# A graph network on one core: split-precision attention scores, a full-precision second weight layer on row halves, softmax numbers stored in rows of 512, and an earlier scatter of the carries

## What is computed

```python
wk = mlp2(edge_features, k_w1, k_b1, k_w2, k_b2)     # relu(x @ w1 + b1) @ w2 + b2
wv = mlp2(edge_features, v_w1, v_b1, v_w2, v_b2)
k = tensor_product(x_dst, edge_sh, wk, Cqk)          # sum_s sh[e,s] * (x_e @ C[:,s,:]) * w
v = tensor_product(x_dst, edge_sh, wv, Cv)
attn = einsum('ehd,ehd->eh', q[edge_src], k)         # 8 heads of 16
ex = exp(attn - segment_max(attn)[edge_src])
alpha = ex / (segment_sum(ex)[edge_src] + 1e-16)
upd = segment_sum(v * alpha) @ W_out
out = batchnorm(x @ W_self + upd)                    # then a residual and a layer norm
```

## Time and profile before

| | before |
|---|---|
| median of 3 runs | 2948.41 us (2947.21 to 2949.53) |
| profiled execution: time, span | 2947.53 us, 2945.7 us |
| mean granted TensorE clock over the span | 0.899 |
| busy in the span: PE, DVE, ACT, POOL | 2469.1, 2612.7, 1514.6, 1731.3 us |

### The profile page before, as it was taken

One profiled execution on the slowest core, in us unless ns is written; L12 is line 12 of the kernel. 1 busy time (PEld: TensorE's weight loads), 2 busy tenths in 40 slices (PEclk: granted clock), 3 DMA queues, 4 the chain that ended last, 5 costly groups with the idle time before them and its releaser, 6 DMA issues.

```text
span 2945.7 us, 48186 instructions
## 1 busy us (share of the span) xinstructions
PE 2469.1 (84%) x12310; PEld 1787.3 (61%) x12505; DVE 2612.7 (89%) x3389; ACT 1514.6 (51%) x2914; POOL 1731.3 (59%) x1719
## 2 busy tenths in 40 slices
PE   2233347999999999999999999999999999999714
PEld 1233315677777776777677776777677777777511
DVE  6688835899999999999999999999999999999737
ACT  1321224566666655666566665666566566666310
POOL 1800037777777766667676666666666677665030
PEclk7555557999999999999999999999999999999855
DMA  6787714245555544444444444444445544544340
GB/s 187 202 222 187 210 25 111 76 131 149 148 149 145 148 147 139 141 142 148 139 144 142 146 147 140 140 144 147 142 141 147 148 141 142 148 144 132 121 124 11
DMA packets 282407, 415.35 MB, mean 141 GB/s; under 512 B 64463, under 2 KB 191875, under 8 KB 278470
## 3 DMA queue, kind: packets, MB, share of 16 engines
q1 hardware_dynamic: 222278, 296.67, 32.4%
q0 software_dynamic: 52704, 107.19, 15.1%
q10 hardware_dynamic: 7128, 8.13, 0.8%
HBM read 309.59 MB, written 102.20 MB: 140 GB/s over the span
## 4 chain that ended last, share of the span: by engine, by line
PE 52%; DVE 7%; issue 6%; ACT 3%; DMA 2%; POOL 2%; SPq 0%; DVEq 0%; ACTq 0%; POOLq 0%
PE bank L1118 11%; PE bank L1120 9%; PE bank L1119 9%; PE bank L1142 5%; PE bank L1163 4%; PE bank L1194 2%; PE bank L1124 2%; PE bank L1125 2%; PE bank L1095 2%; PE bank L1113 2%; DVE xa_t L1538 1%; DVE z_l L1546 1%; PE bank L1102 1%; POOL gathered L745 1%; PE bank L1101 1%
## 5 line engine op out<-in xcount | busy, mean ns | idle before, releaser
L745 POOL DMA_INDIRECT gathered<-xtab_d,src_g x784 | 780.6, 996 | 449.7 <-PE bank L1095 203.0
L745 POOL DMA_INDIRECT gathered<-qtab_d,dst_g x784 | 801.9, 1023 | 257.2 <-issue 249.0
L1118 PE MATMUL bank<-z_h,wt_h 128*128 128x512 f32 x1568 | 729.6, 465 | 27.9 <-DVE val L1578 27.9
L1538 DVE TENSOR_TENSOR xa_t<-bank,r_r 128x512 f32<-128x512 f32 x980 | 667.3, 683 | 13.5 <-PE bank L1142 10.3
L876 ACT ACTIVATE z_h<-xa_t 128x512 fp32r<-128x512 f32 x980 | 617.4, 634 | 110.1 <-DVE xa_t L1538 100.3
L1120 PE MATMUL bank<-z_h,wt_l 128*128 128x512 f32 x1568 | 620.7, 396 | 0.0
L1119 PE MATMUL bank<-z_l,wt_h 128*128 128x512 f32 x1568 | 618.8, 395 | 0.0
L1546 DVE TENSOR_TENSOR z_l<-xa_t,z_h 128x1024 fp32r<-128x1024 f32 x392 | 478.0, 1219 | 48.2 <-ACT z_h L876 44.6
L1118 PEld LDWEIGHTS bank<-z_h,wt_h 128*128 128x128 f32 x1568 | 301.1, 192 | 131.4 <-issue 92.7
L869 ACT ACTIVATE hid<-bank,b1kv 128x512 f32<-128x512 f32 x196 | 134.8, 688 | 476.4 <-PE bank L1102 462.4
L1120 PEld LDWEIGHTS bank<-z_h,wt_l 128*128 128x128 f32 x1568 | 294.9, 188 | 69.2
(11 more groups left out here) (222 smaller groups left out, 4057.9 us busy)
## 6 DMA issues: line engine op xcount, KB each, us to landing
nrow_d<-x_r SPq DMA_DIRECT2D x196, 288.0 KB
ea<-in_ea_t SPq DMA_DIRECT2D x392, 128.0 KB
exb<-exd_d SPq DMA_DIRECT2D x392, 128.0 KB
dmb<-exd_d SPq DMA_DIRECT2D x392, 128.0 KB
ea_c<-in_ea_t SPq DMA_DIRECT2D x49, 512.0 KB, 5.0
aggrow_d<-xa_t SPq DMA_DIRECT2D x49, 512.0 KB, 3.9
gathered<-xtab_d,src_g POOLq DMA_INDIRECT x784
gathered<-qtab_d,dst_g POOLq DMA_INDIRECT x784
```

Of the source, the lines that this page charges most:

```text
L745: rows_in = pool.indirect_dma_start(rows[:, c % 4, k, :], None, table, bass.IndirectOffsetOnAxis(ap=picked[:, s, at:at + 1], axis=0))
L1118: pe.matmul(ps[:, :], wt_h[rows, w, :], high, start=start, stop=False)
L1538: dve.tensor_tensor(z[:, i, :], bank[2 + (NJ * c + i) % 2][:, :], xt[:, c % 2, :], ALU.mult).then_inc(z_ok, 1)
```

## The change

1. **Second weight layer.** `weights` no longer uses rounded parts. Two plain fp32 matmuls of 256 edges for the keys and two for the values, in turn, replace the six rounded ones of 512. `hid_h` (ScalarE) and `hid_l` (VectorE) are gone, and the matmuls wait for `hid` alone.
2. **Scores.** `kq` is now split: `scores_high` (ScalarE, new) rounds it to `kq_h`, `scores_low` (VectorE, new) takes the remainder `kq_l`, and four rounded matmuls of 256 replace two plain fp32 ones. `kq` has one buffer in place of two.
3. **Softmax numbers.** The rows of the batch are ordered half first, then group, then head. `exd_d` holds rows of 512. A batch is stored by four DMAs of 56 rows (before: two of 112), and a group's `exb` and `dmb` are loaded by two DMAs with rows of 512 (before: four with rows of 256). The reset flags are loaded by two DMAs per batch (before: one).
4. **Tail.** The carries are scattered after 12 of the 25 gathers (before: 16).

```diff
@@ tiles
-        kq = in_h(P, 2 * G).rearrange("p (b g) -> p b g", b=2)
+        kq = in_h(P, G)
...
@@ load_rs
-                sp.dma_start(rs_b[:, s % 2, :], ... .to_broadcast([NPC, H, HG])).then_inc(rs_in[s % 2], 16)
+                for f in range(2):
+                    sp.dma_start(rs_b[f * BG * H:(f + 1) * BG * H, s % 2, :], flags[f].to_broadcast([BG, H, HG])
+                                 ).then_inc(rs_in[s % 2], 16)
@@ store_exponents
                 for k, tile in enumerate((b_att, b_dec)):
-                    sp.dma_start(exd_d[bass.ds(j * (UNROLL // BG) + s, 1), k].rearrange("o i f h w -> (o i f h) w"),
-                                 tile).then_inc(exd_out[s % 2], 16)
+                    for f in range(2):
+                        sp.dma_start(exd_d[bass.ds(j * (UNROLL // BG) + s, 1), k, :, :, f * HG:(f + 1) * HG]
+                                     .rearrange("o g h w -> (o g h) w"), tile[f * BG * H:(f + 1) * BG * H, :]
+                                     ).then_inc(exd_out[s % 2], 16)
@@ load_exponents
                 for k, tile in enumerate((exb, dmb)):
-                    for f in range(2):
-                        sp.dma_start(tile[:, c % 2, f * HG:(f + 1) * HG], ... .to_broadcast([H, DH, HG]))
+                    sp.dma_start(tile[:, c % 2, :], ... .to_broadcast([H, DH, G])).then_inc(exd_in[c % 2], 16)
@@ tail, GpSimd
-            gather_ends(range(0, 16))
+            gather_ends(range(0, 12))
...
-            gather_ends(range(16, NT))
+            gather_ends(range(12, NT))
@@ ScalarE
-                act.activation(hid_h[:, :], ps_hw[:, :], ACT.Relu, bias=b1kv[:, :]).then_inc(hid_ok, 1)
+            def scores_high(j, c):
+                done(act, kq_ok, j, c)
+                past(act, att_ps, j, c, 1)
+                act.activation(kq_h[:, :], kq, ACT.Copy).then_inc(kqh_ok, 1)
@@ TensorE, weights
-                done(pe, hidl_ok, j, c)
+                done(pe, hid_ok, j, c)
...
-                for ps, rows, done_ps in ((ps_xw, slice(0, D), wk_ps), (ps_hw, slice(D, P), wv_ps)):
-                    split_matmul(ps, W2KV, hid_h[rows, :], hid_l[rows, :], True, True, rows).then_inc(done_ps, 1)
+                for f in range(2):
+                    edges = slice(f * HG, (f + 1) * HG)
+                    mk = pe.matmul(ps_xw[:, edges], w2kv[0:D, :], hid[0:D, edges], start=True, stop=True)
+                    mv = pe.matmul(ps_hw[:, edges], w2kv[D:P, :], hid[D:P, edges], start=True, stop=True)
@@ TensorE, scores
-                done(pe, kq_ok, j, c)
+                done(pe, kql_ok, j, c)
...
-                    mm = pe.matmul(ps_att[0:BP, 0:HG], head_sel[:, BP - H - H * i:2 * BP - H - H * i],
-                                   kq[:, c % 2, f * HG:(f + 1) * HG], start=i == 0, stop=i == NPC - 1)
+                    for part in (kq_h, kq_l):
+                        mm = pe.matmul(ps_att[0:BP, 0:HG], head_sel[:, BP - H - H * i:2 * BP - H - H * i],
+                                       part[:, f * HG:(f + 1) * HG], ...)
@@ VectorE
-                dve.tensor_tensor(hid_l[:, :], hid[:, :], hid_h[:, :].bitcast(F32), ALU.subtract
-                                  ).then_inc(hidl_ok, 1)
-                past(dve, att_ps, j, c, 2)
-                dve.tensor_tensor(kq[:, c % 2, :], ps_k[:, :], qt[:, c % 2, :], ALU.mult).then_inc(kq_ok, 1)
+                past(dve, kql_ok, j, c, 1)
+                dve.tensor_tensor(kq, ps_k[:, :], qt[:, c % 2, :], ALU.mult).then_inc(kq_ok, 1)
+            def scores_low(j, c):
+                done(dve, kqh_ok, j, c)
+                past(dve, att_ps, j, c, 1)
+                dve.tensor_tensor(kq_l[:, :], kq, kq_h[:, :].bitcast(F32), ALU.subtract).then_inc(kql_ok, 1)
```

More of the change, by code:

```diff
@@ L27 @@
 NJ = 5
-CK, CV, W2KV, W1KV = 0, NJ, 2 * NJ, 2 * NJ + 1
-NW = 2 * NJ + 2
+CK, CV, W1KV = 0, NJ, 2 * NJ
+NW = 2 * NJ + 1
 H = 8
@@ L82, in gnn_two_layers @@
         nrow_d = dram("nrow_d", [EP, RW])
-        exd_d = dram("exd_d", [NB, 2, BG, 2, H, HG])
+        exd_d = dram("exd_d", [NB, 2, BG, H, G])
         carry_d = dram("carry_d", [NP + PIECES, RW])
@@ L102, in gnn_two_layers @@
         wt_l = sb("wt_l", [P, NW, O], F32R)
-        head_sel = sb("head_sel", [P, 2 * BP - H])
+        w2kv = sb("w2kv", [P, O])
+        head_sel = sb("head_sel", [P, 2 * BP - H], F32R)
         chain_cut = sb("chain_cut", [P, PIECES])
@@ L228, in gnn_two_layers @@
         hid = sb("hid", [P, G])
-        hid_h = sb("hid_h", [P, G], F32R)
-        hid_l = sb("hid_l", [P, G], F32R)
+        kq_h = sb("kq_h", [P, G], F32R)
+        kq_l = sb("kq_l", [P, G], F32R)
         qt = sb("qt", [P, 2, G])
@@ L398, in gnn_two_layers @@
         zl_ok = sem("zl_ok")
-        hidl_ok = sem("hidl_ok")
         wth_ok = sem("wth_ok")
@@ L403, in gnn_two_layers @@
         kq_ok = sem("kq_ok")
+        kqh_ok = sem("kqh_ok")
+        kql_ok = sem("kql_ok")
         val_ok = sem("val_ok")
@@ L603, in load_exponents @@
                 hold()
-                sp.wait_ge(exd_out[c // BG % 2], j * (UNROLL // BG // 2 * 32) + (c // BG // 2 + 1) * 32)
+                sp.wait_ge(exd_out[c // BG % 2], j * (UNROLL // BG // 2 * 64) + (c // BG // 2 + 1) * 64)
                 hold()
                 for k, tile in enumerate((exb, dmb)):
-                    for f in range(2):
-                        sp.dma_start(tile[:, c % 2, f * HG:(f + 1) * HG],
-                                     exd_d[bass.ds(j * (UNROLL // BG) + c // BG, 1), k, c % BG, f]
-                                     .rearrange("o h w -> (o h) w").rearrange("h (o w) -> h o w", o=1)
-                                     .to_broadcast([H, DH, HG])).then_inc(exd_in[c % 2], 16)
+                    sp.dma_start(tile[:, c % 2, :],
+                                 exd_d[bass.ds(j * (UNROLL // BG) + c // BG, 1), k, c % BG]
+                                 .rearrange("o h w -> (o h) w").rearrange("h (o w) -> h o w", o=1)
+                                 .to_broadcast([H, DH, G])).then_inc(exd_in[c % 2], 16)
             def store_row(j, c):
@@ L915, in rows @@
                 done_batch(act, bturn_ok, j, c // BG, 4)
-                act.activation(row[:, c % 2, :, O:RW],
-                               b_turn[:, c // BG % 2, c % BG * 2:c % BG * 2 + 2, :, :]
-                               .rearrange("p f h w -> p (f h) w"), ACT.Copy).then_inc(row_ok, 1)
+                act.activation(row[:, c % 2, :, O:RW].rearrange("p (f h) w -> p f h w", f=2),
+                               b_turn[:, c // BG % 2, bass.ds(c % BG, 2, BG), :, :], ACT.Copy).then_inc(row_ok, 1)
             def body(j, c):
@@ L938, in body @@
                     batch_turned(j, s)
+                if live(j, c - 1):
+                    scores_high(j, c - 1)
                 if live(j, c + 1):
@@ L1161, in scores @@
                 for f in range(2):
-                    i = c % BG * 2 + f
-                    mm = pe.matmul(ps_att[0:BP, 0:HG], head_sel[:, BP - H - H * i:2 * BP - H - H * i],
-                                   kq[:, c % 2, f * HG:(f + 1) * HG], start=i == 0, stop=i == NPC - 1)
+                    i = f * BG + c % BG
+                    for part in (kq_h, kq_l):
+                        mm = pe.matmul(ps_att[0:BP, 0:HG], head_sel[:, BP - H - H * i:2 * BP - H - H * i],
+                                       part[:, f * HG:(f + 1) * HG], start=c % BG == 0 and f == 0 and part is kq_h,
+                                       stop=c % BG == BG - 1 and f == 1 and part is kq_l)
                 mm.then_inc(att_ps, 1)
@@ L1555, in edge_low @@
                                   ALU.subtract).then_inc(eal_ok, 1)
-            def hidden_low(j, c):
-                done(dve, hid_ok, j, c, 2)
-                past(dve, wv_ps, j, c, 1)
-                dve.tensor_tensor(hid_l[:, :], hid[:, :], hid_h[:, :].bitcast(F32), ALU.subtract
-                                  ).then_inc(hidl_ok, 1)
             def key_query(j, c):
@@ L1607, in weigh_values @@
             def weigh_values(j, c):
-                landed(dve, exd_in, j, c, 64)
+                landed(dve, exd_in, j, c, 32)
                 done(dve, val_ok, j, c)
@@ L1642, in body @@
                     batch_sums(j, s)
+                if live(j, c - 1):
+                    scores_low(j, c - 1)
                 if live(j, c + 1):
```

19 lines of the change are left out of this document (9 added, 10 removed).

## The result

The change takes the median from 2947.9 to 2942.4 us: 5.5 us less, ratio 0.9978, 95% interval [0.9969, 0.9987]. The prediction was 38 us off, to 2910, so the direction was right and the size was seven times too big. The profiled execution of after took 2940.88 us.

What follows compares the result with a forecast made beforehand. TensorE was taken to bound most of the loop, with VectorE close behind; 28 us in the loop, 5 in the drain and 5 in the tail came off the profiled 2947.5, giving a median of 2910 us, range 2886 to 2943.

Steps and rivals of the forecast that it cites:

- Scores and weights: TensorE's body: score matmuls of 0.12 save 0.38 us, the second weight layer costs 0.16 more, 11.43 to 11.21.
- The strict order: Weight layer: matmuls start strictly in program order, five slots, +0.22 us; in a rival at 2938 us, chance 0.14.
- the lost overlap: Rival, weight layer: plain fp32 doesn't overlap on row halves, TensorE's body 12.08, 3036 us; chance 0.15.
- In the batch's third body that room is taken: ScalarE: batch evacuations fill its idle room, so the new 0.6 us rounding pushes `wv` and two `z_h` back.
- VectorE becomes the bound: Rival, loop: `key_query` wait and ScalarE's delay take the slack, bodies near 11.3, gain 11 us, 2927; chance 0.13.
- The wait at `key_query`: VectorE, ordinary bodies: a new wait of about 0.1 us for the weights, coming out of 0.31 of slack.
- nothing moves, by some other wait in the loop: Rival, loop: some other wait eats the gain, time near 2946 us; chance 0.03.
- Softmax numbers in the drain: End of loop: two loads a group instead of four make six rounds shorter, 5 us gained (1 to 8).
- The 1.0 a round: End of loop: gain taken for each of six rounds, 6 us in all, less 0.85 for two more stores.
- Tail: After the loop: four gathers go behind the scatter, which starts 5.0 us earlier; gain 5 us, or 3.
- 28 + 5 + 5: Whole kernel: 28 us from the loop (1.0 per batch), 5 from the drain, 5 from the tail; 38 in all.
- strict order or slow loads: Rival, TensorE: five weight slots or score matmuls 0.177 apart, body near 11.43, only ends gain, 2938; chance 0.14.

Runs made afterwards that it cites:

- `only_scores`: The kernel before with the split scores alone (hid_h and hid_l stay): 2996.54 us, ratio 1.0168.
- `only_weights`: The kernel before with the fp32 second weight layer alone: 2965.33 us, ratio 1.0059.
- run 1: The changed kernel with scores_high moved ahead of batch_turned on ScalarE: 2936.15 us, ratio 0.9956.
- run 3, the two moves: The changed kernel with scores_high ahead of batch_turned on ScalarE and scores_low ahead of key_query on VectorE: 2929.35 us, ratio 0.9935.
- Run 2: The changed kernel with only scores_low moved ahead of key_query on VectorE: 2951.96 us, ratio 1.0022.
- the control: The kernel before with three gathers of x rows per group in place of four (output incomplete): 2943.88 us, ratio 0.9988.
- run 7: The changed kernel with scores_high and scores_low moved earlier and three gathers of x rows per group in place of four (output incomplete): 2909.29 us, ratio 0.9870.
- run 5: The changed kernel with three gathers of x rows per group in place of four (output incomplete): 2922.31 us, ratio 0.9913.
- run 15: The changed kernel with scores_high and scores_low moved earlier and each 128x1024 z_l subtraction made as two of 128x512 side by side: 2906.85 us, ratio 0.9868.

## Why the prediction missed by its size

**Scores and weights: right.** Slots of 0.12 (forecast 0.12), keys and values in pairs, the body 11.21 (forecast 11.21). The strict order and the lost overlap didn't happen, and `only_scores` and `only_weights` have the bodies that these terms give.

**VectorE and ScalarE: the first step that failed.** "In the batch's third body that room is taken", it would push things back, and the price "up to 0.5 per batch, 14 us in all", if the cover of the longer TensorE body were gone, was named and then put at nothing in the sum. It stood in the rival "VectorE becomes the bound" alone (chance 0.13). The cover was not there. The timeline of after in that body:

```profile
2406.72 0.73 ACT L913 ACTIVATE h_all<-bank 128x112 f32<-128x112 f32 x4 [2.64 <-PE bank L1191]
...
2407.31 0.65 ACT L889 ACTIVATE kq_h<-h_all 128x512 fp32r<-128x512 f32 x1
...
2407.99 0.69 DVE L1591 TENSOR_TENSOR kq_l<-h_all,kq_h 128x512 fp32r<-128x512 f32 x1 [0.60 <-ACT kq_h L889]
```

`kq_h` waits for `batch_turned`, which waits 2.64 us for TensorE's transposes, and VectorE waits 0.60 for `kq_h`, in a stretch in which VectorE is behind. A seven is 81.27, not 80.7: 0.5 to 0.6 a batch, about 15 us, as priced. The run that moves `scores_high` brings it back (80.8). The rest of that rival did not come: ordinary bodies are 11.21 and not 11.3.

**The wait at `key_query`: size off, effect nil.** It was 0.34 us in 79 bodies where 0.1 was forecast, but with `kq_l` moved ahead of it clean sevens go from 80.8 (run 1) to 80.7 (run 3) only, so in them it was slack for the most part. Run 2 can't tell, since the move brings 39 us more of waiting for `kq_h`.

**GpSimd: the step that wasn't there, the other half of the loss.** "Most of the loop is TensorE's, then, but VectorE is close behind" left out the engine that was 59% busy. Its need was never worked out: 8 x (1.01 + 0.30) = 10.5 us a group before, and it looked safe against 11.21. But the duration of a gather is not fixed. Before, GpSimd started its x gathers when `x_turn` ended, at the same place of every body. In the change gathers take 1.13, GpSimd needs 11.4 and more, and no longer waits. Then q rows come late, as here in the timeline of after:

```profile
1036.40 0.94 POOL L749 DMA_INDIRECT gathered<-xtab_d,src_g  x1 [0.30 <-issue]
...
1037.67 0.63 PE L1122 MATMUL bank<-ident,gathered 128*128 128x128 f32 x4 [0.98 <-DMA gathered<-qtab_d,dst_g]
1038.31 1.21 DVE L1628 TENSOR_TENSOR_SCAN x_r<-dmb,val 128x512 f32<-128x512 f32 x1
1038.92 1.36 POOL L749 DMA_INDIRECT gathered<-qtab_d,dst_g  x1 [0.31 <-issue]
1039.48 1.23 DVE L1561 TENSOR_TENSOR z_l<-xa_t,z_h 128x1024 fp32r<-128x1024 f32 x1
...
1045.11 1.22 DVE L1561 TENSOR_TENSOR z_l<-xa_t,z_h 128x1024 fp32r<-128x1024 f32 x1
1045.72 1.43 POOL L749 DMA_INDIRECT gathered<-xtab_d,src_g  x1 [0.30 <-issue]
```

The gather at 1038.92 begins while VectorE is in the scan (`x_r`, to 1039.52) and ends at 1040.28; the one at 1045.72 begins in a `z_l` (to 1046.33) and ends at 1047.15; the first one in the fence begins in neither and takes 0.94. This is the whole of the lengthening. In the trace of after, from 560 to 2760 us, 696 gathers last over 1.0 us, and each of them ends 0.75 to 0.85 us behind the end of an operation of VectorE that has no operand in PSUM; in before it is all 246. The time above 0.94 adds up to 95 us in before and to 276 in after, and that difference is the 180 us by which GpSimd is busier. Behind `z_l` it went from 62 to 134, behind the scan from 11 to 61, and behind the subtraction that the change moved from 0.2 (`hid_l`) to 52 (`kq_l`). The operations are as long as before: the gathers now begin at other points of VectorE's order, and more of them (932 for 704) begin inside such an operation.

Removing one gather in eight brings back 2291.2 - 2273.7 = 17.5 us of the loop; the control's loop is 5.3 shorter as well, so 12 are GpSimd's (17 by the medians: 20 less the control's 3). This is the rival "nothing moves, by some other wait in the loop", which had a chance of 0.03.

**Softmax numbers in the drain: the term of 5 us was nothing.** The two loads with twice the bytes land 5.05 to 5.16 us behind the last issue where it took 3.73, and a round takes 7.92 for 7.79. The 1.0 a round that the sum had is the term that failed. The lower bound of the sum (a gain of 0.4 a round if the bytes set the pace) was the nearer one.

**Tail: right.** 4.9 us by the trace of the change, 5.5 in the run with it alone, forecast 5.

**The sum.** 28 + 5 + 5 was forecast. Measured: of the 28, 13 to 16 went to the `kq_h` wait (run 7 against run 5) and 12 to 17 to GpSimd, together all of it; the drain gave 0; the tail 5. With `scores_high` and `scores_low` moved and GpSimd relieved, the loop gives its 28.0. The rival nearest by its number, 2938 ("strict order or slow loads", only the ends gain), is so by luck: its mechanism did not occur, and the ends gave 5 of the 10 us that it took for them.

## What to carry to other kernels

Work out what every engine needs per round of the loop, also one that is 59% busy, and see which waits keep it in step: an engine whose wait rows vanish after a change is a candidate for the new bound, and a run that gives it less to do tells. The duration of a GpSimd gather is a result, not a constant: when VectorE's work shifts against it, price it again by where the gathers begin, and try several short VectorE operations beside it in place of a long one (27 us in one kernel here, about nothing in another). A conditional price that the text names ("if that cover were gone") has to be checked in the very body in which the cover is thinnest.

## What the runs showed of the hardware

- **Gathers and VectorE.** A gather that begins while VectorE is in an operation whose operands are all in SBUF, and of which more than 0.13 us are left, ends 0.82 us behind that operation's end (0.75 behind a scan): in all 19 traces of this study every gather over 1.0 us ends 0.75 to 0.85 behind one. A gather that begins in an operation with an operand in PSUM is not lengthened: 359 of them in after take 0.94 to 0.97. And one that has begun 0.19 us ahead of the operation isn't either. Both cases, from before: begun 0.06 us behind the start of a `z_l`, a gather takes 1.95; begun 0.19 ahead of it, 0.94.

```profile
2406.80 1.19 DVE L1546 TENSOR_TENSOR z_l<-xa_t,z_h 128x1024 fp32r<-128x1024 f32 x1
2406.86 1.95 POOL L745 DMA_INDIRECT gathered<-xtab_d,src_g  x1 [0.30 <-issue]
```

```profile
2370.85 0.94 POOL L745 DMA_INDIRECT gathered<-xtab_d,src_g  x1 [0.30 <-issue]
2371.04 1.22 DVE L1546 TENSOR_TENSOR z_l<-xa_t,z_h 128x1024 fp32r<-128x1024 f32 x1 [0.18 <-ACT z_h L876]
```

 The Trainium skill ("SBUF — State Buffer", section "SBUF: two separate sides") says that VectorE and GpSimd share a pair of SBUF ports that one of them locks for a whole instruction, and that a DMA issued by GpSimd then can't have its descriptors written. The trace agrees: the gather waits for the end of the instruction, and the 0.82 us behind it are nearly its whole 0.94. That only the first 0.15 us or so of a gather are exposed is an estimate from these rows. In the other direction no lengthening shows: a `z_l` takes 1.19 to 1.29 us in every trace in which it is whole.
- **Shorter operations.** With the operations of 1.22 us halved, bytes unchanged, the mean gather went from 1.13 us to 1.01 on top of the two moves, from 1.13 to 1.03 on the change, and from 1.01 to 1.03 on before. What counts is how much of an operation is left when a gather begins, so the places count as well as the lengths. Side by side (run 15), a gather that begins in the first half ends 0.82 us behind that half, and not behind the second, in 139 of 155 cases.
- **Order of matmuls.** Plain fp32 matmuls of keys and values on the two row halves, issued in turn, start 0.01 us apart and overlap in full: from the first pair (2299.34) to the product behind the last (2300.41) it is 1.07 us, where the six rounded ones took 0.91, and the 0.16 more is what was forecast for the case of a full overlap.
- **Fewer, bigger loads gained nothing here.** The last of two loads of 256 KB (rows of 512, broadcast) takes 5.05 to 5.16 us in the chain behind its issue, the last of four of 128 KB took 3.73: the 1.3 us of issuing that were saved came back in the landing.
